# A one-column GpSimd write, waited for, behind each gather of neighbour rows

## The chip, the cores and the metric

The kernel runs on one core of one Trainium2 chip. The metric is the device time of one execution in microseconds; before the change it is 3226.21 us, the median of 3 runs (3226.19 to 3241.27). A core has five engines with queues of their own: TensorE (PE; its weight loads are listed as PEld), VectorE (DVE), ScalarE (ACT), GpSimd (POOL) and SyncE (SP). They are ordered against one another by semaphores alone. DMAs are issued by SP, ScalarE and GpSimd and moved by 16 DMA engines.

## What is computed

A layer over 12500 nodes with 256 features, in float32. The graph has 212500 edges, sorted by destination.

```python
xn = layernorm(x)
# graph part: weighted sum of neighbour rows, two products, leaky ReLU, row norm
n  = segment_sum(edge_weight[:, None] * xn[src], dst)
g  = leaky(xn @ W1.T + b1 + (n + n * xn) @ W2.T + b2);  g = g / max(norm(g), 1e-12)
# mixing part: one k'v product over all nodes per head, then a two-layer product
q, k, v = split(xn @ w_qkv + b_qkv);  k, v = ln(k), ln(v)
m  = gelu((q @ (k.T @ v / N) + xn) @ w1 + b1) @ w2 + b2 + xn
x  = x + g + m
# experts: each node goes to its best of 8 experts (256 -> 1024 -> 256), scaled
x  = x + prob * expert[argmax(gate(layernorm(x)))](layernorm(x))
```

## The kernel before

The work lies in three layers that run over one another.

**Neighbour sums.** The edges are padded and cut into columns of 128 edges; four columns are a group (GROUP = 4), two groups a pair. There are 1664 columns, 416 groups and 208 pairs (PAIRS). For each column GpSimd issues one indirect DMA that fetches 128 rows of xn, 1 KB each, from device memory into a slot of rows_sb (L677, in gather_group). rows_sb has 24 slots (ROW_SLOTS), which is three pairs. Before it gathers group g, GpSimd waits until TensorE has multiplied the pair that used the slots (pair_mm, three pairs back). VectorE builds for each pair the matrices s_sb of weights by position (L1109, L1111). TensorE multiplies a pair (multiply_pair, L735): it waits for s_sb, for the rows of both groups (row_ld) and for ScalarE to have copied the pair before out of the PSUM bank (pair_copied). ScalarE copies the result to sums (L1480, waits for pair_mm), TensorE turns it (turn_pair, L744), and VectorE adds it to acc (L1127).

**Dense work beside it.** Each pair p has a place in one order that all engines follow. In the first 48 places stand the key/value steps (TensorE L755, L763, L765, L770; ScalarE L1489, L1495, L1498; VectorE L1142 to L1147). After a short fold, one tile of 128 nodes after another enters the per-tile chain: hidden product (TensorE L808, signal c_h_mm), mixing and graph product (L818 to L825, signal c_mm), leaky ReLU and norms on VectorE (L1198 and following) and ScalarE (L1511 to L1535), gate logits and routing. ScalarE's L1511 and VectorE's L1198 wait for c_mm.

**Expert units.** As soon as enough nodes are routed, units of 256 nodes run in between: GpSimd fetches their rows (gather_unit, L693, two DMAs), TensorE multiplies (L893, L903, L922), ScalarE and VectorE finish (L1554, L1561, L1339 to L1350), and GpSimd adds the result to the output with an indirect DMA (scatter_unit, L703, two DMAs). 56 units make 112 DMAs of each kind. Part of them runs under the neighbour gathers, the rest after them.

GpSimd's program for a place is: the pair's first group of four gathers, gathers of units that stand at this place, the second group, then scatters of units. TensorE's program for a place is: multiply the pair, turn the pair before, then the steps of the place. Both are written in this order and an engine does not leave it.

flag_f is a 128x1 tensor; it holds a flag that VectorE computes and TensorE and VectorE read before the gathers start, and nobody reads it after flag_done. pool_seq is a semaphore that no instruction of this kernel uses. GpSimd's other compute instructions are constants at the start (L627 to L647).

Of the kernel before, what the change touches and what calls it, by code (L numbers as in the profile page):

```python
# [29 lines left out]
def build(nc, x, src, dst, weight, dst_grouped, gnn_w1t, gnn_b1, gnn_w2t, gnn_b2,  # L30
# [37 lines left out]
    with ctx:  # L68
        def sb(name, shape, dt=F32):
            return ctx.enter_context(nc.sbuf_tensor(name, shape, dt))  # L70

        def sem(name):
            return ctx.enter_context(nc.semaphore(name))
# [27 lines left out]
        flag_f, flag_i = sb("flag_f", [P, 1]), sb("flag_i", [1, 1], I32)  # L101
# [153 lines left out]
        pool_seq, dve_seq, act_seq = sem("pool_seq"), sem("dve_seq"), sem("act_seq")  # L255
# [370 lines left out]
        def gpsimd_program(pool):  # L626
# [46 lines left out]
            def gather_group(g):  # L673
                if g >= ROW_SLOTS // GROUP:
                    pool.wait_ge(pair_mm, (g - ROW_SLOTS // GROUP) // 2 + 1)
                for c in range(g * GROUP, (g + 1) * GROUP):
                    pool.indirect_dma_start(  # L677
                        out=rows_sb[:, c % ROW_SLOTS, :], out_offset=None, in_=xn_d,
                        in_offset=bass.IndirectOffsetOnAxis(ap=src_sb[:, c:c + 1], axis=0)
                    ).then_inc(row_ld[g % len(row_ld)], 16)  # L680

            def gather_unit(k):
                b = batch_of[k]
                tokens = min((routes[b][-1] + 1) * P, N)
                if k == 0 or batch_of[k - 1] != b:
                    pool.wait_ge(q_ready, sum(units_after(i) > units_after(i - 1) for i in range(b + 1)))
                    for t in range(max(0, routes[b][-1] + 1 - OS), routes[b][-1] + 1):
                        pool.wait_ge(c_st[t % OS], 32 * (t // OS + 1))
                if k >= 2:
                    pool.wait_ge(x_turned, k - 1)  # L690
                for i in range(UNIT_TILES):
                    col = k * UNIT_TILES + i
                    pool.indirect_dma_start(  # L693
                        out=xs[:, k % 2 * UNIT_TILES + i, :], out_offset=None, in_=h2_d[0:tokens, :],
                        in_offset=bass.IndirectOffsetOnAxis(ap=gat_i[:, col:col + 1], axis=0)
                    ).then_inc(xs_ld[k % 2], 16)
# [11 lines left out]
            for p in range(PLACES):  # L708
                if p < PAIRS:
                    gather_group(2 * p)  # L710
                for k in gather_at[p]:
                    gather_unit(k)
                if p < PAIRS:
                    gather_group(2 * p + 1)
                for k in scatter_at[p]:
                    scatter_unit(k)
# [870 lines left out]
        block = ctx.enter_context(nc.Block())  # L1587
        block.sync(sync_program)
        block.gpsimd(gpsimd_program)
        block.tensor(tensor_program)  # L1590
        block.vector(vector_program)
# [66 lines left out]
```

## Time and profile before

| | |
|---|---|
| median of 3 runs | 3226.21 us |
| profiled execution: time | 3227.74 us |
| profiled execution: span, first to last instruction | 3226.0 us |
| TensorE busy | 2391.7 us, 74% |
| GpSimd busy | 1931.6 us, 60% |
| VectorE busy | 1537.6 us, 48% |
| ScalarE busy | 932.3 us, 29% |
| mean granted TensorE clock | 0.874 of full |

A row of the timeline gives the start in us from the span's start, the duration, the engine, the line and operation, what is written from what, and in square brackets how long the engine had been idle and what ended that. "issue" is time in which the engine waited for nothing that the profile shows; "remote", or "another core or an unknown queue", is a wait whose end no instruction of the profile accounts for. Several instructions of one line may be merged in a row (x16). The ends of matmuls are modelled. Of an indirect DMA the GpSimd row covers the making of the transfer's descriptors, and not the transfer.

### The profile page before, as it was taken

What the parts mean: (1) busy time and instruction counts of PE and PEld (TensorE: products, weight loads), DVE (VectorE), ACT (ScalarE), POOL (GpSimd) and SP (SyncE); (2) the same over time, 40 slices, a digit from 0 to 9 for tenths busy, and PEclk for the clock granted to TensorE, in tenths of its full rate; (3) what the DMA queues carried; (4) which work ended last, traced back from release to release, by engine and by line L of the source; (5) the groups of instructions that cost most, each with busy time, mean ns of one, the idle gap of its engine ahead of it and who ended that gap; (6) DMA issues with size and microseconds to landing.
All of it is one profiled execution on the core that took longest, in us unless ns stands there. A gap on an engine that the chain in (4) does not pass through costs nothing.

```text
span 3226.0 us, 40169 instructions
## 1 busy us (share of the span) xinstructions
PE 2391.7 (74%) x11900; PEld 1748.9 (54%) x11900; DVE 1537.6 (48%) x4468; ACT 932.3 (29%) x2125; POOL 1931.6 (60%) x1905
## 2 busy tenths in 40 slices
PE   0277777765677778887788887777778678588998
PEld 0134444433555556665566665556556456477887
DVE  7466666652465555554344344344344344344222
ACT  4122222211333434332232232223232222232332
POOL 0466666666666666666666666666666666623332
PEclk9999999987788878888989888898888788798999
DMA  9644444434454565555555555555554554535663
GB/s 284 189 134 137 133 139 134 134 113 121 145 151 145 155 202 157 168 170 153 173 171 164 168 172 153 161 166 163 155 158 121 168 147 125 166 99 156 185 182 98
DMA packets 361873, 501.49 MB, mean 155 GB/s; under 512 B 58585, under 2 KB 289487, under 8 KB 361553
## 3 DMA queue, kind: packets, MB, share of 16 engines
q0 software_dynamic: 101376, 243.85, 28.2%
q1 hardware_dynamic: 219394, 216.65, 21.3%
q10 hardware_dynamic: 40886, 38.41, 3.6%
q8 instruction: 99, 1.62, 0.2%
q14 instruction: 118, 0.96, 0.1%
HBM read 436.45 MB, written 66.01 MB: 156 GB/s over the span
## 4 chain that ended last, share of the span: by engine, by line
PE 43%; another core or an unknown queue 22%; issue 14%; DVE 10%; ACT 7%; DVEq 2%; DMA 1%; ACTq 1%; SPq 0%; POOL 0%; POOLq 0%
PE bank L903 9%; PE bank L922 9%; PE bank L735 6%; PE bank L765 5%; PE bank L808 2%; PE bank L820 2%; PE bank L825 2%; PE bank L823 2%; DVEq L1125 1%; PE bank L744 1%; PE bank L869 1%; DVE arena L1142 1%; PE bank L763 1%; ACT L1526 1%
## 5 line engine op out<-in xcount | busy, mean ns | idle before, releaser
L677 POOL DMA_INDIRECT rows_sb<-xn_scratch,src_sb x1664 | 1638.6, 985 | 954.2 <-issue 554.7
L735 PE MATMUL bank<-rows_sb,s_sb 128*48 128x256 f32 x3328 | 466.0, 408 | 159.6 <-issue 83.6
L903 PE MATMUL bank<-acc 128*128 128x256 f32 x1792 | 469.6, 409 | 33.5 <-issue 20.2
L922 PE MATMUL bank<-acc 128*128 128x256 f32 x1792 | 466.5, 405 | 30.7 <-issue 17.0
L735 PEld LDWEIGHTS bank<-rows_sb,s_sb 128*48 128x48 f32 x3328 | 218.0, 129 | 363.4 <-issue 227.2
L922 PEld LDWEIGHTS bank<-acc 128*128 128x128 f32 x1792 | 362.2, 206 | 96.6 <-issue 25.4
L903 PEld LDWEIGHTS bank<-acc 128*128 128x128 f32 x1792 | 359.9, 205 | 95.6 <-issue 45.7
L1554 ACT ACTIVATE acc<-bank,acc 128x256 f32<-128x256 f32 x448 | 187.8, 471 | 521.2 <-PE bank L903 255.1
L703 POOL DMA_INDIRECT out_dram<-acc,sca_i x112 | 179.5, 1603 | 256.0 <-DVE acc L1350 228.5
L1480 ACT COPY sums<-bank 112x256 f32<-112x256 f32 x208 | 77.5, 372 | 791.6 <-remote 704.5
L808 PE MATMUL bank<-arena,weff 128*128 128x128 f32 (+1 forms) x784 | 145.5, 343 | 129.0 <-issue 70.4
L1127 DVE TENSOR_TENSOR acc<-acc,bank 128x96 f32 x416 | 106.0, 255 | 255.7 <-issue 152.3
L808 PEld LDWEIGHTS bank<-arena,weff 128*128 128x128 f32 x784 | 132.1, 248 | 147.9 <-issue 145.2
L765 PE MATMUL bank<-arena 128*128 128x512 f32 x392 | 208.6, 659 | 0.0
L1511 ACT ACT_TABLE_LOAD x95 | 121.9, 1283 | 290.1 <-remote 166.9
L1198 DVE TENSOR_SCALAR arena<-bank 128x256 f32<-128x256 f32 x98 | 41.5, 424 | 336.1 <-remote 268.1
L744 PE MATMUL bank<-ident,sums 112*128 112x112 f32 x416 | 89.9, 299 | 139.1 <-DVE acc L1127 72.1
L744 PEld LDWEIGHTS bank<-ident,sums 112*128 112x128 f32 x416 | 44.9, 149 | 235.1 <-issue 225.0
L693 POOL DMA_INDIRECT acc<-h_scratch,gat_i x112 | 111.0, 991 | 76.5 <-issue 31.6
L763 PE MATMUL bank<-bkv_hl,ones_r 128*128 128x512 f32 x98 | 47.7, 487 | 137.0 <-DVE arena L1142 112.2
L820 PE MATMUL bank<-w2m_sb,arena 128*128 128x256 f32 x392 | 133.5, 475 | 0.4 <-issue 0.4
L1511 ACT ACTIVATE arena<-bank,beff 128x128 f32<-128x128 f32 x196 | 61.3, 364 | 246.0 <-remote 229.5
(208 smaller groups left out, 3425.9 us busy)
## 6 DMA issues: line engine op xcount, KB each, us to landing
acc<-ffn_w_in SPq DMA_DIRECT2D x112, 1024.0 KB
rows_sb<-xn_scratch,src_sb POOLq DMA_INDIRECT x1664
arena<-xn_scratch SPq DMA_DIRECT2D x194, 128.0 KB
xnt_scratch<-arena SPq DMA_DIRECT2D x97, 128.0 KB
arena<-xnt_scratch SPq DMA_DIRECT2D x97, 128.0 KB
arena<-x_in SPq DMA_DIRECT2D x97, 128.0 KB
h_scratch<-arena ACTq DMA_DIRECT2D x97, 128.0 KB
out_dram<-arena ACTq DMA_DIRECT2D x97, 128.0 KB
```

The lines of the kernel that those rows point to most:

```text
L677: pool.indirect_dma_start(out=rows_sb[:, c % ROW_SLOTS, :], out_offset=None, in_=xn_d, in_offset=bass.IndirectOffsetOnAxis(ap=src_sb[:, c: ...
L693: pool.indirect_dma_start(out=xs[:, k % 2 * UNIT_TILES + i, :], out_offset=None, in_=h2_d[0:tokens, :], in_offset=bass.IndirectOffsetOnAxi ...
L703: pool.indirect_dma_start(out=out[0:tokens, :], out_offset=bass.IndirectOffsetOnAxis(ap=sca_i[:, col:col + 1], axis=0), in_=yo[:, k % YS * ...
L735: m = pe.matmul(psum[0][i * HALF:i * HALF + WIN, 0:D], s_sb[:, p % S_SLOTS, i * GROUP + j, :], rows_sb[:, c % ROW_SLOTS, :], start=j == 0, ...
L744: m = pe.transpose(psum[7][:, h * P:h * P + HALF + WIN], sums[:, p % SUM_SLOTS, h * P:(h + 1) * P], ident[0:HALF + WIN, 0:HALF + WIN])
L765: m = pe.matmul(kv[0:r, :], xnt[:, t % R1, h, 0:r], wkv_sb[:, h, :], start=False, stop=h == H - 1)
L808: m = pe.matmul(psum[2][:, f * P:f * P + r], weff[:, h, f * P:(f + 1) * P], c_xnt[:, t % XS, h, 0:r], start=h == 0, stop=h == H - 1)
L820: pe.matmul(mix, c_hid[:, par, f, 0:r], w2m_sb[:, f, :], start=False, stop=f == H - 1)
L903: m = pe.matmul(bank[:, i * UNIT:(i + 1) * UNIT], w1_sb[k % 2][:, h, f * P:(f + 1) * P], xt[:, k % 2, h, :], start=h == 0, stop=h == H - 1)
L922: m = pe.matmul(bank[:, i * D:(i + 1) * D], hid[:, f, i * P:(i + 1) * P], w2_sb[k % 2][:, f, :], start=f == 0 and i == 0, stop=f == FC - 1 ...
L1511: act.activation(c_hid[:, par, f, 0:r], psum[2][:, f * P:f * P + r], ACT.Gelu, bias=beff[:, f:f + 1]).then_inc(c_gelu, 1)
L1554: act.activation(hid[:, f, :], bank[:, i * UNIT:(i + 1) * UNIT], ACT.Relu, bias=b1_sb[k % 2][:, f:f + 1]).then_inc(l1_relu, 1)
```

## The change

Behind every gather of neighbour rows GpSimd writes zero to flag_f (128 partitions, one column), and that write adds one to pool_seq; then GpSimd waits until pool_seq has reached the number of gathers so far. The gathers and scatters of the units have nothing added. No other engine's program is changed, and no order.

```diff
                         out=rows_sb[:, c % ROW_SLOTS, :], out_offset=None, in_=xn_d,
                         in_offset=bass.IndirectOffsetOnAxis(ap=src_sb[:, c:c + 1], axis=0)
                     ).then_inc(row_ld[g % len(row_ld)], 16)
+                    pool.memset(flag_f[:, :], 0.0).then_inc(pool_seq, 1)
+                    pool.wait_ge(pool_seq, c + 1)
```

## Rows read from the trace of the kernel before

**Rows 1.** The page: span, and the chain that ended last by engine:

```profile
span 3226.0 us, 40169 instructions
...
PE 43%; another core or an unknown queue 22%; issue 14%; DVE 10%; ACT 7%; DVEq 2%; DMA 1%; ACTq 1%; SPq 0%; POOL 0%; POOLq 0%
```

**Rows 2.** Busy us and counts by stage; then the clock, DMA share, GB/s:

```profile
145.00:700.00 555.00, 407.64 (x1904) 221.65 (x1906) 357.35 (x683) 117.46 (x338) 373.12 (x372) 0.93 0.48 133
700.00:2832.00 2132.00, 1615.04 (x8226) 1211.45 (x8223) 960.44 (x3140) 642.19 (x1408) 1409.91 (x1399) 0.84 0.53 157
2832.00:3226.00 394.00, 355.63 (x1722) 309.84 (x1721) 133.04 (x340) 127.10 (x292) 115.42 (x88) 0.94 0.52 145
```

**Rows 3.** GpSimd by line: busy us, mean ns, then idle us before:

```profile
L677 POOL DMA_INDIRECT rows_sb<-xn_scratch,src_sb x1664 | 1638.6, 985 | 954.2 <-issue 554.7 <-remote 223.3 <-PE bank L735 176.2
...
L629 POOL MEMSET nil<- 128x1 f32 x1 | 0.1, 101 | 0.0
```

**Rows 4.** What GpSimd waited for, 145 to 700 us: total us, times, longest:

```profile
POOL rows_sb L677 <- issue: 99.8, 326, 0.4
POOL rows_sb L677 <- remote: 69.0, 40, 4.1
POOL rows_sb L677 <- PE bank L735: 13.4, 6, 3.0
```

**Rows 5.** The same waits, 700 to 2832 us:

```profile
POOL rows_sb L677 <- issue: 344.5, 1129, 0.4
POOL rows_sb L677 <- PE bank L735: 162.8, 55, 6.8
POOL rows_sb L677 <- remote: 154.2, 79, 4.4
```

**Rows 6.** Timeline, all engines: start us, us, engine line, [idle before <-releaser]:

```profile
407.51 1.93 PE L735 MATMUL bank<-rows_sb,s_sb 128*48 128x256 f32 x16
...
418.06 1.93 PE L735 MATMUL bank<-rows_sb,s_sb 128*48 128x256 f32 x16
...
421.22 0.96 POOL L677 DMA_INDIRECT rows_sb<-xn_scratch,src_sb  x1 [0.31 <-issue]
...
421.60 1.88 PE L765 MATMUL bank<-arena 128*128 128x512 f32 x4
...
422.48 1.02 POOL L677 DMA_INDIRECT rows_sb<-xn_scratch,src_sb  x1 [0.30 <-issue]
...
425.07 0.37 ACT L1480 COPY sums<-bank 112x256 f32<-112x256 f32 x1 [6.05 <-remote]
425.31 0.95 POOL L677 DMA_INDIRECT rows_sb<-xn_scratch,src_sb  x1 [1.81 <-remote]
```

**Rows 7.** Timeline near 1045 us, in the later stage:

```profile
1043.03 1.03 PE L825 MATMUL bank<-w2g_sb,arena 128*128 128x256 f32 x4
...
1048.10 0.42 DVE L1198 TENSOR_SCALAR arena<-bank 128x256 f32<-128x256 f32 x1 [1.13 <-remote]
1048.14 1.28 ACT L1511 ACT_TABLE_LOAD   x1 [7.78 <-remote]
1048.49 0.95 POOL L677 DMA_INDIRECT rows_sb<-xn_scratch,src_sb  x1 [2.22 <-remote]
```

**Rows 8.** GpSimd's timeline at the start: writes in a row, one wait:

```profile
1.35 0.20 POOL L634 MEMSET ident<- 128x128 f32 x1
1.50 0.20 POOL L635 MEMSET ones<- 128x128 f32 x1
1.85 0.29 POOL L637 TENSOR_SCALAR_AFFINE_SELECT ident<-ident 128x128 f32<-128x128 f32 x1 [0.16 <-POOL ones L635]
```

**Rows 9.** Timeline after the last neighbour gather:

```profile
3004.15 0.73 DVE L1350 COPY_PREDICATED acc<-acc 128x512 f32<-128x512 int32 x1
...
3005.71 1.62 POOL L703 DMA_INDIRECT out_dram<-acc,sca_i  x1 [8.13 <-DVE acc L1350]
```

**Rows 10.** A VectorE instruction that reads and writes SBUF, by line:

```profile
L1220 DVE TENSOR_SCALAR arena<-arena,c_stat,c_rstd 128x256 f32<-128x256 f32 x98 | 41.9, 428 | 3.6
```

## The prediction, made before the changed kernel had run

> **What bounds the kernel now.** Read in this order: the chain of the page, the table by stage, GpSimd's lines and waits, then two short timelines. The profiled execution has a span of 3226.0 us and a time of 3227.7 us, 1.5 us above the median of 3226.2 us; the sum below is made against the span, and the difference is carried unchanged.
>
> The chain gives TensorE 43% and "another core or an unknown queue" 22% [rows 1]. There is one core, so the second share has to be explained. The stages are: 145 to 700 us, neighbour gathers beside the key/value work; 700 to 2832 us, gathers beside the per-tile chain and the expert units; 2832 us to the end, units alone [rows 2]. In the last stage TensorE is busy 355.6 of 394 us and no neighbour gather runs, so the change does not touch it.
>
> In the first stage GpSimd is busy 373.1 us, sits 99.8 us between gathers ("issue", 0.30 us at a time) and 82.4 us in 46 waits for TensorE's pair signal [rows 2, 4]: 555.3 of 555 us. Nothing is left over. In the second stage it is 1409.9 busy + 344.5 issue + 317.0 in 134 waits = 2071 of 2132 us, and the missing 61 us are starts and waits of the units' own transfers [rows 2, 5]. So GpSimd is occupied all through both stages, and only its waits for the pair signal are slack, if they are slack at all.
>
> They look self-made. GpSimd may run three pairs ahead of TensorE. The pair's matmuls start at 418.06 us and are drawn as over after 1.93 us, at 419.99; later matmuls (L765, 421.60) follow. Yet ScalarE's copy and GpSimd's next gather, which both wait for that pair signal, start only at 425.07 and 425.31 us, 5.1 us after the drawn end [rows 6]. In the later stage three engines wake together: L825 is drawn as over at 1044.06, and VectorE, ScalarE and GpSimd start at 1048.10, 1048.14 and 1048.49 us [rows 7]. At 425 us the signal came 1.6 us after the last gather had ended (422.48 + 1.02 = 423.50). After 2832 us, without neighbour gathers, no such share of the chain appears. My reading: while gathers follow one another without a pause, TensorE's signals arrive late, and GpSimd's stop at the end of a pair lets them through. This is an inference; the drawn end of a matmul is a model.
>
> **What the change adds.** 1664 writes of one column and 1664 waits, one behind each L677 [rows 3]. Nothing is removed and no other engine has a new instruction. Behind the waiting GpSimd stands the next gather, or a unit's gather or scatter; TensorE waits for those rows three pairs later, VectorE and ScalarE for TensorE. That GpSimd waits three pairs ahead gives no cover, since it is full.
>
> *Price of one.* Today a gather starts 0.30 us after the one before has ended, and 1.26 us after its start (421.22 to 422.48) [rows 3, 6]. With the change that gap holds: the time s until the write starts, the write, and the time from its signal to the next gather's start.
> - The write: a 128x1 write took 0.10 us [rows 3].
> - Signal to gather: ScalarE's copy and the gather wait for the same signal, and the gather starts 0.24 us later (425.07, 425.31) [rows 6]. The nearest row below is 0.15 us, from a write's end (1.70) to the dependent instruction's start [rows 8]. The farthest above is 0.83 us, from L1350's end (3004.88) to a scatter's start (3005.71) [rows 9]; a scatter is a longer instruction with another releaser, so I take 0.25.
> - s: zero if the write is already queued, 0.30 if it needs as long as a gather does now. Small instructions in a row start before their predecessor has ended [rows 8], so it lies near the low end: 0.10.
>
> Added: 0.10 + 0.10 + 0.25 - 0.30 = 0.15 us. The ends are 0 + 0.10 + 0.15 - 0.30 = -0.05, which I cut at zero because a waited-for instruction can't shorten the gap by itself, and 0.30 + 0.10 + 0.83 - 0.30 = 0.93 us. With the gather's own 0.25 and the largest s it is 0.35 us, my working upper end.
>
> The GPSIMD Engine Reference of the Trainium skill (Instruction dispatch) says that an instruction that writes is complete only when its data has landed for all eight cores. The sum would be the same by it, unless that landing is slow behind a gather's own writes, which no row of this trace shows.
>
> *What it does to the time.* 1664 x 0.15 = 250 us of GpSimd time: about 60 us in the 400 gathers of the first stage and its start, 190 us in the 1264 of the second. If the late signals stay as they are, the 1.8 us stop at a pair's end (82.4 / 46) stays too, and the first stage pays 60 us in full. In the second stage part of the 317 us is TensorE's honest lateness (it is busy 1615 of 2132 us), and a slower GpSimd finds some pairs ready: I let a third of 190, 63 us, disappear there. Sum: 60 + 127 = +187 us.
>
> The write also competes with VectorE. A gather of 1.02 us stands beside one of 0.96, and L1220 reads and writes SBUF for 0.43 us, 98 times [rows 6, 10]; I set no term for it, since it is 42 us of 2132, and 2% of 1264 writes held for 0.2 us come to 5 us. SBUF — State Buffer of the Trainium skill (Who interferes with whom) speaks against the change here: a VectorE instruction in a 2-port mode and a GpSimd instruction exclude one another for their whole length. By that rule the sum would be those 5 us higher, by the row alone zero.
>
> **Rivals.**
> 1. *The signals stay late (the forecast): +187 us, about 3413 us.* For it: the release at 425 us needed 1.6 us without a gather, and a gap that grows from 0.30 to 0.45 us is far from that. The 46 waits of the first stage come to 1.8 us each, so the stop is a regular one.
> 2. *The write and its wait let TensorE's signals through at every gather.* Then GpSimd's stops shrink: 82 us in the first stage, and three quarters of 317 = 238 us in the second, against 250 us added: -70 us. ScalarE's copy and the per-tile chain start earlier as well; for that I take 5% of the 517 us in which TensorE is not busy in the second stage, 25 us: -95 us, 3131 us. It decides in favour of faster when one write and wait cost under (82 + 238) / 1664 = 0.19 us. For it: the lateness exists only beside gathers, and a write that has to land before the next gather begins is a real pause of that kind. In the first stage TensorE's own step allows it: its pairs at 407.51 and 418.06 us are 10.55 us apart, under the present 555 / 46.5 = 11.9 us a pair. Against it: no row shows a release in a short gap.
> 3. *Relief and price cancel*: relief as in 2 with 0.25 us each, 416 - 320 - 90 = about 0, 3226 us.
> 4. *A dear write*: no relief and 0.35 us each: 582 - 100 = +480 us, about 3710 us; with 0.93 us it would be 4700 us and more.
> 5. *The change does nothing*, because GpSimd's wait is always over in time. It isn't possible with GpSimd full, unless the added part of the gap is near zero: 3226 to 3235 us. I count it with 3.
>
> **How the numbers follow.** Case 1: 0.45; case 2: 0.34; cases 3 and 5: 0.09; case 4: 0.12. The single forecast is case 1, 3413 us. A measurement of this kernel can tell about 0.5% (16 us) from no change. Faster: case 2, 0.33 after a sliver that falls within 0.5%; within 0.5%: 0.10; slower: cases 1 and 4, 0.57. The range goes from 3095 us, below the centre of case 2 with less than one chance in ten beneath it, to 3640 us, which holds case 1 with up to 0.30 us for a write and wait less 80 us absorbed, and leaves out most of case 4. The likeliest case's own range is 3300 to 3600 us (0.07 to 0.28 us each).
>
> **What would show it.** In the profile of the changed kernel: 1664 more GpSimd writes of about 0.1 us; start-to-start of two gathers at 1.41 us (below 1.35 or above 1.55 my price is wrong). For case 1: the pair signal still arrives in the stop at the pair's end, GpSimd's waits on TensorE in the first stage stay near 80 us, and the unknown share of the chain stays near 20%. For case 2: those waits fall under 30 us, ScalarE's copy follows the pair's matmuls within 0.1 us, and the unknown share falls below 8%. The last stage, from the last neighbour gather to the end, keeps its length near 394 us in every case; if it doesn't, the sum leaves something out. The forecast is wrong if the late signals are not tied to the density of gathers but to what GpSimd does between them, because then the length of the gap, on which I decided between 1 and 2, says nothing.

## The result: 1.9% slower, and the profile after

The changed kernel took 3293.4 us (median of 4 runs), beside 3230.3 us for the kernel before (4 runs): a ratio of 1.0191, 95% interval [1.0157, 1.0225], 63 us. The forecast was +187 us: the right direction, three times the size. The ratios here and below are the recorded ones with their intervals; they can lie up to 0.3% off the quotient of the two medians given beside them. Behind line 680 the line numbers of the changed kernel are two higher (L735 is now L737).

The page's chain by engine, after:

```profile
span 3286.8 us, 42230 instructions
...
PE 43%; issue 18%; another core or an unknown queue 15%; DVE 14%; ACT 4%; DVEq 2%; DMA 2%; POOL 1%; ACTq 0%; POOLq 0%; SPq 0%
```

The unknown share was 22% before [rows 1] and is 15%: between the 20% and the 8% that the prediction had set as the marks of its first and second case. GpSimd's lines (busy, mean ns of one | idle before them and what ended most of it):

```profile
L677 POOL DMA_INDIRECT rows_sb<-xn_scratch,src_sb x1664 | 1652.4, 993 | 791.3 <-issue 315.2 <-POOL flag_f L681 240.9 <-PE bank L737 119.7
L681 POOL MEMSET flag_f<- 128x1 f32 x1664 | 195.9, 118 | 1.7
```

GpSimd's waits from 145 to 700 us, then from 700 to 2832 us (total us, times, longest):

```profile
POOL rows_sb L677 <- POOL flag_f L681: 59.9, 221, 0.3
POOL rows_sb L677 <- issue: 39.1, 128, 1.8
POOL rows_sb L677 <- PE bank L737: 19.8, 7, 5.3
POOL rows_sb L677 <- remote: 16.0, 8, 3.1
```

```profile
POOL rows_sb L677 <- POOL flag_f L681: 169.9, 612, 0.9
POOL rows_sb L677 <- issue: 168.7, 547, 9.6
POOL rows_sb L677 <- PE bank L737: 99.8, 33, 8.0
POOL rows_sb L677 <- remote: 93.5, 44, 3.8
```

"remote" and "PE bank L737" together are the stops for the pair signal. In the first stage there are 15 of 35.8 us in all, where there were 46 of 82.4 [rows 4]; in the second 77 of 193.3 us, where there were 134 of 317.0 [rows 5] (the gathers now run on to 2891 us, and 6 us of stops lie behind 2832). Two sums over the gathers alone show where the time went:

- *GpSimd's own work and gaps.* Before: 1638.6 busy + 452.8 "issue" (554.7 less 101.9 at the start) = 2091 us [rows 3]. After: 1652.4 + 195.9 + 213.6 (315.2 less 101.6 at the start) + 240.9 = 2303 us. By this sum 1664 writes and waits cost 212 us, 0.127 us each.
- *Stops for TensorE.* Before: 223.3 + 176.2 = 399.5 us. After: 119.7 + 115.6 = 235.3 us. So 164 us of stops are gone.

The stops in the whole run (total us, times, longest), before and after:

```profile
POOL rows_sb L677 <- remote: 223.3, 119, 4.4
POOL rows_sb L677 <- PE bank L735: 176.2, 61, 6.8
```

```profile
POOL rows_sb L677 <- PE bank L737: 119.7, 40, 8.0
POOL rows_sb L677 <- remote: 115.6, 55, 3.8
```

Both sums are somewhat too high, and by the same amount, because a stop also holds the 0.30 us gap that would stand there anyway. There were 180 stops and are 95, so about 85 x 0.30 = 26 us have only moved from the second heading to the first. Without them it is about 186 us of price, 0.11 us each, and about 138 us of relief (estimates from these rows). The difference is +48 us either way. The other 13 of the span's +60.8 us lie in the units' transfers. The scatters alone sat idle 256.0 us before and 271.3 us after: where one stands behind a waited write it starts some 0.8 us after it (15 waits, 12.4 us), and all their waits other than for VectorE went from 27.2 to 49.3 us.

The table by stage, cut where the first stage and the gathers end in this run, has the last stage at 396 us against 394 before [rows 2]; its columns are the stretch, its length, and each engine's busy time:

```profile
105.00:715.00 610.00, 418.00 (x1936) 227.52 (x1936) 366.51 (x700) 123.58 (x342) 463.23 (x800) 0.92 0.46 132
715.00:2891.00 2176.00, 1618.21 (x8229) 1195.33 (x8230) 961.20 (x3153) 646.26 (x1409) 1556.13 (x2662) 0.83 0.52 153
2891.00:3287.00 396.00, 357.79 (x1735) 311.08 (x1733) 132.37 (x339) 127.03 (x292) 118.60 (x90) 0.95 0.52 145
```

### The profile page after: what moved, and what is told of

Read it like the earlier page. It is cut to its first block, busy times and chain, and to the rows that moved or that the text cites. A ratio compares the mean times of both kernels' runs of the same rounds, so it can differ in the third digit from the quotient of the medians.

```text
span 3286.8 us, 42230 instructions
## 1 busy us (share of the span) xinstructions
PE 2394.6 (73%) x11900; PEld 1734.0 (53%) x11900; DVE 1533.0 (47%) x4468; ACT 940.9 (29%) x2125; POOL 2140.6 (65%) x3569
## 4 chain that ended last, share of the span: by engine, by line
PE 43%; issue 18%; another core or an unknown queue 15%; DVE 14%; ACT 4%; DVEq 2%; DMA 2%; POOL 1%; ACTq 0%; POOLq 0%; SPq 0%
PE bank L924 10%; PE bank L905 9%; PE bank L737 7%; PE bank L767 3%; PE bank L810 2%; DVEq L1127 2%; PE bank L822 2%; PE bank L827 2%; PE bank L825 2%; DVE arena L1144 1%; PE bank L746 1%; DVE arena L1148 1%; DVE arena L1149 1%; DVE s_sb L1111 1%
## 5 line engine op out<-in xcount | busy, mean ns | idle before, releaser
L677 POOL DMA_INDIRECT rows_sb<-xn_scratch,src_sb x1664 | 1652.4, 993 | 791.3 <-issue 315.2
L737 PE MATMUL bank<-rows_sb,s_sb 128*48 128x256 f32 x3328 | 484.9, 412 | 162.7 <-issue 94.0
L737 PEld LDWEIGHTS bank<-rows_sb,s_sb 128*48 128x48 f32 x3328 | 220.7, 130 | 388.3 <-issue 255.8
L705 POOL DMA_INDIRECT out_dram<-acc,sca_i x112 | 180.1, 1608 | 271.3 <-DVE acc L1352 221.6
L681 POOL MEMSET flag_f<- 128x1 f32 x1664 | 195.9, 118 | 1.7
L1497 ACT ACTIVATE arena<-bank 128x512 f32<-128x512 f32 x98 | 58.7, 599 | 318.3 <-PE bank L767 215.3
```

Of the source, the lines that this page charges most:

```text
L677: pool.indirect_dma_start(out=rows_sb[:, c % ROW_SLOTS, :], out_offset=None, in_=xn_d, in_offset=bass.IndirectOffsetOnAxis(ap=src_sb[:, c: ...
L681: pool.memset(flag_f[:, :], 0.0).then_inc(pool_seq, 1)
L705: pool.indirect_dma_start(out=out[0:tokens, :], out_offset=bass.IndirectOffsetOnAxis(ap=sca_i[:, col:col + 1], axis=0), in_=yo[:, k % YS * ...
L737: m = pe.matmul(psum[0][i * HALF:i * HALF + WIN, 0:D], s_sb[:, p % S_SLOTS, i * GROUP + j, :], rows_sb[:, c % ROW_SLOTS, :], start=j == 0, ...
```

## The experiments

**How to read their times.** A diff of a kernel with writes of flag_f is shown against the changed kernel (h2's against the kernel before), the others against the kernel before. The same kernel before had two times here, each steady within its group of runs: 2841 to 2854 us in the groups of e, h and i, and medians of 3233 to 3238 us in those of f and g, like the 3226 to 3230 us of the first runs. It isn't tied to a chip's number as recorded: f, g and i carry the same one. I call them the *prompt* and the *late* condition, for what the traces show. In the prompt condition TensorE's signals follow the drawn end of its matmuls and GpSimd hardly ever stops. The traces tell the two apart: over all engines, waits called "remote" come to 2055 us in the trace of before, to 1736 to 2050 us in those of f, g2, g3 and g4 and to 1765 us after the change, and there is not one in the ten traces of e, h and i. The kernel before was traced in the first, late group only. Every ratio is against the kernel before in its own group. The texts on record speak of two kinds of chip; read "condition" there.

The difference itself says what the late condition costs this kernel: 3235 - 2847 = 388 us, and the stops in the trace of before are 399.5 us. e1 and f4, one kernel in either condition, take it apart: the span grows by 386 us, GpSimd's stops by 384 us less 35 us of ordinary gaps that they swallow, and the rest lies in longer gathers (7 us) and the units' transfers.

### e1: the wait moved behind the next gather

```diff
+                    if c:
+                        pool.wait_ge(pool_seq, c)
                     pool.memset(flag_f[:, :], 0.0).then_inc(pool_seq, 1)
-                    pool.wait_ge(pool_seq, c + 1)
```

> The write stays behind every gather, but GpSimd waits for the write of the gather before, which is long over. Theory P (the added time is a price per gather, paid for waiting until the write is over): the gap between gathers goes back near 0.30 us and the time to that of before, 3225 to 3245 us. Rival R (the write as such costs, waited for or not): spacing stays at 1.34 us and the time at 3280 to 3300 us. Rival L (a write that lands between gathers lets TensorE's late signals through, without the wait as well): GpSimd's waits on TensorE fall as in the changed kernel (399 to 235 us) but without its price, 3100 to 3190 us.

Prompt condition: 2850.4 against 2846.8 us, ratio 1.0007 [0.9997, 1.0018]. The write is there 1664 times and costs nothing. GpSimd's rows and the pair's matmuls (start, length):

```profile
404.64 0.12 POOL L683 MEMSET flag_f<- 128x1 f32 x1
...
404.83 1.93 PE L738 MATMUL bank<-rows_sb,s_sb 128*48 128x256 f32 x16
...
404.95 1.34 POOL L677 DMA_INDIRECT rows_sb<-xn_scratch,src_sb  x1 [0.19 <-issue]
...
406.81 0.37 ACT L1483 COPY sums<-bank 112x256 f32<-112x256 f32 x1 [1.03 <-PE bank L738]
```

The write fills part of the 0.30 us that stood between two gathers anyway: 0.12 written, 0.19 left, 0.31 in all. ScalarE's copy starts 0.05 us after the drawn end (404.83 + 1.93 = 406.76), where in the late trace of before it was 5.1 us [rows 6]. GpSimd's waits in the whole run:

```profile
POOL rows_sb L677 <- issue: 412.1, 1589, 101.8
...
POOL rows_sb L677 <- PE bank L738: 4.7, 20, 0.3
```

### e2: one write and wait behind every fourth gather

```diff
+                    if c % GROUP == GROUP - 1:
-                    pool.memset(flag_f[:, :], 0.0).then_inc(pool_seq, 1)
-                    pool.wait_ge(pool_seq, c + 1)
+                        pool.memset(flag_f[:, :], 0.0).then_inc(pool_seq, 1)
+                        pool.wait_ge(pool_seq, g + 1)
```

> A write and a wait behind every fourth gather only, 416 instead of 1664. Theory P: a quarter of the price, 416 x 0.08 = 33 us, of which GpSimd's shorter stops take back about half: 3240 to 3255 us. Rival L: if one write in four is enough to let the signals through, the stops shrink by some 100 us for 33 us of price: 3140 to 3190 us.

Prompt: 2900.8 us, 1.0201 [1.0173, 1.0229]: 54 us for 416, 0.13 us each, above the 33 us expected. The mean mixes two prices. A gather starts 0.27 us after a write's end (90.8 us in 334 waits), but a unit's scatter 0.83 us (25.7 us in 31), where in e4, without writes, it follows in 0.30; that alone is some 16 of the 54 us. What is left for the other writes is about 0.1 us each, near the corrected account above, with no stops in play.

### e3: two writes, each waited for, behind each gather

```diff
+                    for i in range(2):
-                    pool.memset(flag_f[:, :], 0.0).then_inc(pool_seq, 1)
-                    pool.wait_ge(pool_seq, c + 1)
+                        pool.memset(flag_f[:, :], 0.0).then_inc(pool_seq, 1)
+                        pool.wait_ge(pool_seq, 2 * c + i + 1)
```

> Two writes, each waited for, behind every gather. Theory P: the second pair of write and wait costs more than the first, since nothing of it lies in the gap that was there: a write of 0.11 us and some 0.15 us until the next instruction, 0.25 us x 1664 = 416 us more, at most 100 us of it taken back in stops: 3600 to 3710 us. Rival S (stops take back half of whatever is added, as they did with 0.08 us): 3430 to 3520 us.

Prompt: 3416.9 us, 1.1996 [1.1973, 1.202]: 570 us, 0.34 us a gather. The second one costs 0.34 - 0.13 = 0.21 us, more than the first, which has the old gap to hide in. The 0.34 is again a mean: the next gather starts 0.27 us after the second write inside a group of four, and 0.60 us after it at the first gather of a group (332 row gathers in this trace, all of them the first of their group). Both theories had reckoned from 3230 us, so neither's absolute time applies; only the price can be taken from this run.

### e4: two pairs of row slots in place of three

```diff
-        ROW_SLOTS = 6 * GROUP
+        ROW_SLOTS = 4 * GROUP
```

> The kernel before with 16 instead of 24 row slots, so that GpSimd may run two pairs ahead of TensorE and not three; nothing else is changed. Theory M (GpSimd's stops at a pair's end are made by its own gathers, which keep TensorE's pair signal back until GpSimd is quiet): one signal per stop whatever the lead is, so the first stage keeps its 11.85 us a pair and the whole time stays within 1%, 3200 to 3260 us. Rival H (TensorE is honestly late now and then, and the three pairs of lead cover it): with less lead the stops grow, 3290 us and more.

Prompt: 2871.8 us, 1.0095 [1.007, 1.0119]. With less lead GpSimd stops for 33.9 us where e1's trace has 4.7: with prompt signals the lead is of use.

### f1: the changed kernel once more, in the group that splits it

> The changed kernel itself, beside the kernel before, once more. In the profile of the kernel before GpSimd's stops at a pair's end came to 399 us and took back 164 us of a price of 1664 x 0.127 = 212 us; on the chip of the e runs these stops were 5 us. Theory A (the write and wait cost 0.127 us each wherever they run, and only existing stops can take some of it back): without stops the full price shows, the kernel before + 190 to 230 us; with stops as in the profile of before, + 50 to 80 us. Rival (the difference is a property of the change, not of the stops): + 60 us in either case.

Late: 3291.4 against 3238.0 us, 1.019 [1.0137, 1.0243]. Stops 137.4 + 94.2 = 231.6 us, unknown share 14%: the first result again.

### f2 and f3: the writes in one stage only

```diff
+                    if c < 400:
-                    pool.memset(flag_f[:, :], 0.0).then_inc(pool_seq, 1)
-                    pool.wait_ge(pool_seq, c + 1)
+                        pool.memset(flag_f[:, :], 0.0).then_inc(pool_seq, 1)
+                        pool.wait_ge(pool_seq, c + 1)
```

That is f2; f3 has `c >= 400` and waits for `c - 399`.

> Write and wait behind the first 400 gathers only. Theory A: 400 x 0.127 = 51 us without stops; with stops, of which the first stage has 82 us, + 10 to 25 us.

> Write and wait behind the other 1264 gathers only. Theory A: 1264 x 0.127 = 161 us without stops; with stops + 35 to 60 us. First and later stage together make the whole change, since GpSimd's time adds up; a rival in which an early delay is made good later would leave the sum above the whole.

Late: f2 3250.5 us, 1.0044 [1.0022, 1.0066], +12.5; f3 3275.7 us, 1.0146 [1.0096, 1.0197], +37.7. The parts add up to the whole: 50 against 53 us. The first stage is the telling one, because the prediction gave it no relief. f2's waits there, 145 to 700 us:

```profile
POOL rows_sb L677 <- POOL flag_f L682: 59.7, 220, 0.5
POOL rows_sb L677 <- issue: 37.9, 124, 1.8
POOL rows_sb L677 <- PE bank L738: 25.0, 10, 4.9
POOL rows_sb L677 <- remote: 14.8, 8, 2.3
```

Stops of 39.8 us, against 77.4 (65.8 + 11.6) in the same stretch of f3, which has no writes there. 400 writes at 0.127 us are 51 us (45 us at 0.11), and the time grew by 12.5 us: most of the price comes back at once.

### f4: e1's kernel in the late condition

> The write behind every gather with a wait for the write before it, as e1, beside the changed kernel. Without stops: no change, as e1 (ratio 1.00). With stops as in the profile of before: theory G (stops fall because gathers are spaced wider) says they stay near 400 us and the time is that of the kernel before; rival L (the write lets TensorE's late signals through) says that they fall to some 235 us at no price, and the time falls by 100 to 160 us.

Late: 3239.8 us, 1.002 [0.9996, 1.0045]. GpSimd's waits and its start of a pair:

```profile
POOL rows_sb L677 <- issue: 377.4, 1423, 101.7
...
POOL rows_sb L677 <- remote: 209.1, 118, 4.5
POOL rows_sb L677 <- PE bank L738: 179.2, 63, 6.7
```

```profile
405.15 1.88 PE L768 MATMUL bank<-arena 128*128 128x512 f32 x4
...
407.06 0.60 ACT L1498 ACTIVATE arena<-bank 128x512 f32<-128x512 f32 x1 [3.38 <-PE bank L768]
...
407.18 1.93 PE L738 MATMUL bank<-rows_sb,s_sb 128*48 128x256 f32 x16
...
412.94 0.37 ACT L1483 COPY sums<-bank 112x256 f32<-112x256 f32 x1 [4.80 <-remote]
413.17 0.96 POOL L677 DMA_INDIRECT rows_sb<-xn_scratch,src_sb  x1 [1.25 <-remote]
```

Stops of 388.3 us, as before the change, and the pair's signal 3.8 us late (drawn end 409.11). Not every signal is late: ScalarE's L1498 starts 0.03 us after the drawn end of L768 (405.15 + 1.88 = 407.03), with gathers 1.26 us apart around it. A write behind each gather, by itself, lets nothing through. What relieves needs the wait, or what the wait does: a later start of the next gather.

### g1: e3's kernel in the late condition

> Two writes, each waited for, behind every gather, once more. On the chip where GpSimd had no stops they took 3417 us, 570 us over the kernel before, 0.34 us a gather. Theory T (the stops are slack that a slower GpSimd uses up until nothing of it is left): where stops of some 390 us exist the change is 570 - 350 to 390 us, and the time is the same 3420 to 3470 us as without stops. Rival (only part of the stops can be taken back, as the 164 of 399 us in the changed kernel): 3550 to 3650 us. If this job's chip has no stops: 3410 to 3420 us again.

Late: 3412.6 against 3232.7 us (2 runs), 1.0537 [1.0492, 1.0583]. This is the decisive run. Its time is within 4 us of e3's (3416.9 us), though the kernels before differ by 386 us; theory T had said so, from 3420 us up. The chain, the waits, and a pair's start:

```profile
POOL 62%; issue 22%; PE 11%; DVE 3%; DMA 2%; POOLq 0%; SPq 0%; ACT 0%; DVEq 0%; ACTq 0%
```

```profile
POOL rows_sb L677 <- issue: 488.5, 1076, 101.7
...
POOL rows_sb L677 <- POOL flag_f L682: 200.4, 586, 0.9
```

```profile
404.63 1.93 PE L738 MATMUL bank<-rows_sb,s_sb 128*48 128x256 f32 x16
...
406.61 0.37 ACT L1483 COPY sums<-bank 112x256 f32<-112x256 f32 x1 [1.03 <-PE bank L738]
406.62 0.95 POOL L677 DMA_INDIRECT rows_sb<-xn_scratch,src_sb  x1 [0.27 <-POOL flag_f L682]
...
408.12 1.15 POOL L677 DMA_INDIRECT rows_sb<-xn_scratch,src_sb  x1 [0.27 <-POOL flag_f L682]
...
409.27 0.27 POOL L682 MEMSET flag_f<- 128x1 f32 x2
410.14 0.95 POOL L677 DMA_INDIRECT rows_sb<-xn_scratch,src_sb  x1 [0.60 <-POOL flag_f L682]
```

The chain has no unknown share, GpSimd's stops for the pair signal come to 0.6 us in 2 waits, and the copy starts 0.05 us after the drawn end (406.56). Was this run simply a prompt one? Its trace speaks against it: ten "remote" waits are left on ScalarE and VectorE, 36.1 us in all, where no prompt trace has one. The two largest groups of them:

```profile
ACT L1514 <- remote: 17.5, 2, 9.9
...
DVE arena L1201 <- remote: 13.6, 5, 4.4
```

So the late condition is there and has lost almost all its effect. GpSimd bounds the kernel (62% of the chain, beside 22% of "issue"), and the time is its own need. The gathers are 1.50 us apart as a rule (406.62 to 408.12), 1.83 at the start of a group (the 0.60 us above, 339 times), and 1.61 on the mean; the changed kernel has 1.34 as a rule and 1.40 on the mean, the kernel before 1.26 and 1.29 (stops left out).

### g2: e4's kernel in the late condition

> 16 instead of 24 row slots, once more. Without stops it cost 0.95%. Theory M (the stops are made by GpSimd's own gathers, one a pair, whatever the lead): with stops also within 1% of the kernel before. Rival H (lead covers lateness): with stops 2% slower or more.

Late: 3218.5 us, 0.9938 [0.9915, 0.996], with stops of 218.1 + 202.9 = 421 us. With a third of the lead gone the kernel loses nothing here (it even gains 0.6%), where in the prompt condition it lost 0.95%. So the stops aren't a TensorE that is too slow for GpSimd's lead; the signal is late with 16 slots as with 24.

### g3: quarter rows

```diff
-                        out=rows_sb[:, c % ROW_SLOTS, :], out_offset=None, in_=xn_d,
+                        out=rows_sb[:, c % ROW_SLOTS, 0:64], out_offset=None, in_=xn_d.rearrange("n (a d) -> (n a) d", d=64),
```

One write ahead of the gathers fills the slots with zeros. The kernel leaves out three quarters of each neighbour row, so it computes something else.

> The kernel before, but every gather fetches 256 bytes a row instead of 1 KB, from a view of xn in quarter rows; three quarters of each row are left zero, so the neighbour sums are another computation. GpSimd issues the same 1664 gathers of 128 rows. Theory D (TensorE's signals are kept back by the making of descriptors on GpSimd): where stops exist they stay, 350 us and more, and the time changes by under 1%. Rival X (they are kept back by the bytes that the gathers move): a quarter of the bytes lets them through, the stops fall under 100 us and the time falls towards 2850 to 2950 us.

Late: 3237.1 us, 1.0011 [0.9988, 1.0033], stops 208.3 + 193.7 = 402 us. The run moved 337.9 MB in place of 501.5 MB, and neither time nor stops changed: the lateness isn't the bytes in the row gathers' transfers.

### g4: a wait for landed rows once a pair

```diff
             def gather_group(g):
+                if g >= 2 and g % 2 == 0:
+                    pool.wait_ge(row_ld[(g - 1) % len(row_ld)], 16 * GROUP * ((g - 1) // len(row_ld) + 1))
```

> The kernel before, but GpSimd, before the first group of a pair, waits until the last group that it issued has landed in SBUF, which is a pause at each pair's end by design. Theory Q (where stops exist, they last until the last gather has landed, about 1.6 us after its end, so this wait adds nothing to them): within 1% of the kernel before on such a chip, and on a chip without stops 208 x 1.8 = 370 us slower, which makes it look like the other chip, 3200 to 3240 us. Rival (the stops end for another reason, and the two add up): 200 to 370 us slower where stops exist.

Late: 3282.9 us, 1.0137 [1.0093, 1.018] (2 runs), between what the two theories had said.

```profile
POOL rows_sb L679 <- DMA rows_sb<-xn_scratch,src_sb: 354.2, 146, 6.1
...
POOL rows_sb L679 <- remote: 70.5, 32, 3.2
POOL rows_sb L679 <- PE bank L737: 51.6, 14, 7.1
```

354 us of new waits took the place of 277 us of stops: in all 476 us in place of 399.5. A pause of some 2.4 us, here at 146 of 208 pairs, is mostly used in place of the other one. One long pause a pair moves the stop and doesn't cure it.

### h1 to h3 and i1 to i3: spacing by work, and partial doses

What a wider spacing does and what the wait itself does were still mixed, and so was the longer gap at a group's start. h1 spaces the gathers by a long write without a wait; h2 puts two waited writes behind every second gather; h3 is e2's kernel.

```diff
-        ROW_SLOTS = 6 * GROUP
+        pace = sb("pace", [P, 448])
+        ROW_SLOTS = 4 * GROUP
...
+                    if c:
+                        pool.wait_ge(pool_seq, c)
+                    pool.memset(pace[:, :], 0.0).then_inc(pool_seq, 1)
```

```diff
+                    for i in range(2 * (c % 2)):
+                        pool.memset(flag_f[:, :], 0.0).then_inc(pool_seq, 1)
+                        pool.wait_ge(pool_seq, c + i)
```

> A write of 448 unused columns behind each gather, and no wait for it before the next gather; two pairs of row slots in place of three, for room (that alone gave 3218 against 3233 us). It spaces the gathers by work, not by a wait. Theory G (the spacing of the gathers decides whether TensorE's signals come late): if the row gathers start 1.45 us apart or more, GpSimd's stops for TensorE and for the unknown (before: about 400 us) are under 60 us, TensorE's signals are prompt, and the time is about 2850 us plus 1664 times the spacing over 1.26: 3250 us at 1.50. Rival W (it is GpSimd's waiting for its own write that lets signals through): stops stay at 350 to 430 us at the same spacing, and the time is 3550 to 3650 us. If the write hides beside the gather (spacing up to 1.30), both say stops of 350 us or more and 3210 to 3300 us, and the run tells nothing.

> Two writes, each waited for, behind every second gather only: starts 1.26 and about 1.6 us apart in turn, 1.43 on the mean. Own cost by the chip without late signals (570 us for all): 285 us. If the mean rate over some gathers decides: stops go from 400 to under 120 us, time 3130 to 3250 us, so faster than or level with before. If it is the shortest distance that decides (a dense pair is enough to hold signals back): stops stay over 250 us, time 3380 to 3520 us.

> One write with its wait behind every fourth gather. Own cost 54 us as on the other chip. By the mean rate (1.29 us): stops fall a quarter of the way that the whole change goes (400 to 235), so to 350 to 370 us, time 3240 to 3265 us. If a pause in each group is enough to let signals through (stops under 250 us): 3080 to 3150 us, faster than both kernels. If this chip shows no late signals at all: before 2847, this 2901 us, and the other two kernels tell only their own costs.

This group fell into the prompt condition (before: 2849.2 us), so it tells own costs only: h1 3428.4 us, 1.2035 [1.2015, 1.2055]; h2 3221.9 us, 1.1307 [1.1287, 1.1327]; h3 2905.3 us, 1.0196 [1.0178, 1.0214]. The same three kernels were run again for that reason:

> The kernel of h1 once more, in the hope of a chip on which TensorE's signals come late (before about 3232 us; h1's chip had 2849 and shows only the own cost: 3428 us, gathers 1.61 us apart). On such a chip, theory G (spacing decides): no stops for TensorE or the unknown over 40 us, 3425 to 3440 us. Rival W (GpSimd's wait for its own write lets signals through, and here it waits for none): stops stay at 350 to 430 us, 3750 to 3850 us. On a chip like h1's: 3428 again, nothing told.

> The kernel of h2 once more; its own cost by h2 is 373 us (3222 us on a chip without late signals), the starts of gathers 1.25 and 1.50 us apart and more in turn. On a chip with late signals: if the mean rate decides, stops under 60 us and 3220 to 3290 us; if a dense pair is enough to hold signals back, stops over 200 us and 3420 to 3600 us.

> The kernel of h3 once more; own cost 56 us (2905 us on a chip without late signals). On a chip with late signals: by the mean rate stops of 320 to 370 us and 3225 to 3270 us; if one wait in a group is enough, stops under 200 us and 3080 to 3110 us, faster than both kernels.

Prompt again (before: 2847.5 us): 3426.0, 3215.5 and 2905.2 us, ratios 1.204, 1.1297 and 1.0208. The question is left open. What the six do give, from h1's timeline of GpSimd:

```profile
408.36 0.96 POOL L678 DMA_INDIRECT rows_sb<-xn_scratch,src_sb  x1 [0.16 <-issue]
409.31 0.50 POOL L684 MEMSET pace<- 128x448 f32 x1
409.97 0.96 POOL L678 DMA_INDIRECT rows_sb<-xn_scratch,src_sb  x1 [0.16 <-issue]
```

An unwaited write leaves 0.16 to 0.19 us before the next gather whatever its length (0.12 us in e1, 0.50 us here); a waited one leaves 0.27 us. So the first 0.12 us of unwaited writing are free, and the rest is paid. h2 was dearer than I had worked out: 373 us in place of 285, 0.45 us for each of 832 pairs of writes, where e3's all-over dose costs 0.34. The gap of 0.60 us explains it: it stands before the first gather of a group, 334 times in h2's trace and 332 times in e3's, and every group's end has its pair of writes in both kernels. So h2 saves half of the writes and none of the long gaps. Why two writes make that gap, where one (the changed kernel, e2) leaves 0.27 us, isn't shown.

## Why the prediction was right or wrong, point by point

- **What bounds the kernel: right in the main.** GpSimd is full, and its stops depend on its own pace: they go when it is slower (g1), and less lead doesn't turn them into a loss (g2). But the reading "while gathers follow one another without a pause, TensorE's signals arrive late" names only half of the condition. The prompt groups have the same pace, 1.26 us, and no late signal; something beside the kernel has a part in it. Nor is every signal late (f4's L768).
- **Price of a write and wait: nearly right.** 0.15 us forecast; 0.127 by the account, 0.11 without the gaps that stops had held. The terms can be read in one row pair of after:

```profile
408.67 0.95 POOL L677 DMA_INDIRECT rows_sb<-xn_scratch,src_sb  x1 [0.35 <-issue]
409.63 0.11 POOL L681 MEMSET flag_f<- 128x1 f32 x1
410.01 0.95 POOL L677 DMA_INDIRECT rows_sb<-xn_scratch,src_sb  x1 [0.27 <-issue]
```

  The write starts 0.01 us after the gather's end, not 0.10 (s); it takes 0.11 (0.10 forecast), and the gather starts 0.27 us behind it (0.25 forecast). That makes 0.39 - 0.30 = 0.09 us in such a pair, 1.34 us from start to start, outside the 1.35 to 1.55 that the prediction had allowed. The mean is 1.40 against 1.29 before, since some gathers and gaps are longer. Priced at 0.127, the first term would have been 212 in place of 250 us. For scatters behind a write the prediction had no term; the 0.83 us that it had read from a write's end to a scatter [rows 9] and set aside is what they take (0.8 us), a good part of the 13 us outside the gathers.
- **"Stops absorbed": this is the step that failed.** It had none in the first stage and 63 us in the second. Measured: 47 us (82.4 to 35.8) and 124 us (317.0 to 193.3), by the account of all gathers 164 us (about 138 without the gaps that stops hold). With the right price and this term as forecast the sum would still have been 212 - 63 = +149 us; with both as measured it is +48 us, near the span's +61. The step rested on "a gap that grows from 0.30 to 0.45 us is far from 1.6 us, so the late signals stay as they are". Lateness isn't a yes or no that a single long pause settles: the stops fell from 400 to 235 us with gathers 1.34 us apart as a rule (1.40 on the mean), and to none in g1 (1.50 and 1.61). The right direction owes something to luck: the price came out under the prediction's own turning point of 0.19 us, so with case 2's relief the kernel would have been faster. It was slower because the relief was real but partial, 164 us where case 1 had 63 and case 2 some 320.
- **Rival 2 (the write and wait let signals through): half of it happened.** Its first-stage mark, waits under 30 us, was nearly met (35.8). Its mechanism splits. The write alone lets nothing through (f4). Write and wait together do, in part. Its total failed on size: 235 us of stops are left, where it had 80 or less, and the turning point of 0.19 us by which it would be faster rested on that.
- **Rivals 3 to 5:** relief and price didn't cancel within 0.5%; 0.35 us is what two writes cost on the mean (0.34), not one; and the change isn't free.
- **The write against VectorE:** VectorE is busy 1533.0 us after and 1537.6 before, L681 has a mean of 118 ns, and e1's 1664 unwaited writes cost 0.07%, an interval that holds zero. The term of zero stands. The exclusion between a GpSimd instruction and a VectorE instruction in a 2-port mode that SBUF — State Buffer of the Trainium skill (Who interferes with whom) describes doesn't show in these numbers; no run here was made to single it out.
- **Last stage:** 396 us against 394, as said.

**What is shown and what is not.** Shown: the waits cost 212 us and give back 164 in the late condition (186 and 138 with the gaps set right); a write without its wait does neither; with two waited writes a gather (g1, 2 runs) the stops are gone and the time is that of the prompt condition; in the late condition neither the bytes of a row nor 16 slots in place of 24 raises the time. Not shown: whether it is the distance between gathers, GpSimd's waiting or, in g1, the longer gap at a group's start that frees the signals (h1 and i1 would have told the first two apart in the late condition), why some of TensorE's signals come on time all the same, why only some groups of runs have late signals, and what holds them. The changed kernel itself was not run in the prompt condition; by the 212 us of the account it would take about 2847 + 212 = 3059 us there, an estimate, and lose some 7%. None of the runs beat the kernel before by more than g2's 0.6%, which the prompt condition turns into a loss.

## What to carry to other kernels

When an engine that has no slack gets a wait, first price it by the gap that is there already: an unwaited small instruction may fit into it, a waited one adds its write and its signal's way, less that gap. Price it for each kind of instruction that can stand behind the wait (here 0.27 us to a gather, 0.8 to a scatter), and when you sum idle time by cause, remember that a stop swallows the gap that it replaces. Then ask of each stop on that engine whether it is work that is awaited or a signal that is late, because here the second kind shrank when the engine was slowed, and hid most of the price. Last, run the kernel before in the same group as every variant: here its own time moved by 388 us between groups, six times what the change does.

## What the runs showed of the hardware that I had not expected

- One kernel, two steady times: 2847 us (stops 4.7 us, in e1's near-identical trace) and 3226 to 3238 us (stops 400 us), with no value between them in any group.
- In the late condition the lateness goes with GpSimd's own pace: stops of 400, 235 and 0.6 us with gathers 1.26, 1.34 and 1.50 us apart as a rule (1.29, 1.40 and 1.61 on the mean). Whether the pace or the waiting does it is open.
- After a waited write the next gather starts 0.27 us later, a scatter 0.83 us later (e2). After two waited writes the first gather of a group starts 0.60 us later (332 to 339 times in e3, g1 and h2).
- A gather of 128 rows takes GpSimd 0.95 us and the next starts 0.30 us later, whether a row is 1 KB or 256 B (g3: 1484 gaps, 453.1 us, 0.31 each). A 0.12 us write fits into that gap for nothing.
